# Finer filler, stacks copied by halves and split GpSimd subtractions in a two-layer transformer kernel

## Chip, cores and metric

One core of a Trainium2 chip runs the whole program. The metric is device time in microseconds (us) of one execution; lower is better.

## The reference

Two sequences (batches) of 1024 positions and 512 channels pass through two layers. In each layer both branches read the same normalised input:

```
xn = layernorm(x)
x  = x + causal_attention(xn; Wq, Wk, Wv, Wo) + Wdown(silu(Wgate xn) * (Wup xn))
```

Attention has 16 heads of 32 channels with rotary positions. The feed-forward part (FFN) has 2048 hidden channels in layer 0 and 1408 in layer 1, where its weights are scaled by columns. All is float32. The kernel splits each product into three (high by high, high by low, low by high), each value being held as a rounded high part and a residual low part.

## The kernel before

The order of all work is one list, `STEPS`. Each engine walks it and emits its own part of each step, so the list is the order on every in-order queue, TensorE (PE), VectorE (DVE), ScalarE (ACT), GpSimd (POOL) and SyncE (SP, which issues all DMAs).

The four passes (batch 0 layer 0, batch 0 layer 1, and the same of batch 1) each have an **opening** (normalise and transpose rows 512 to 1023, project the values of all rows and the queries and keys of the first four heads) and four **turns** of four heads each. A turn does, in this order:

- **score stretch one** (`nat` 0 to 15): scores of positions 0 to 511 (half c=0), one matmul each, for four heads. DVE masks and takes the maximum, ACT sums exponentials;
- **score stretch two** (`nat` 16 to 31): half c=1, two matmuls each;
- **weight stretch one** (`st` of sets 0 to 5, with `pv` 0 to 3) and **two** (`st` of sets 6 to 11, `pv` 4 to 9): transposed scores, exponentials by ACT, product with the values, then `wo`;
- the tail, with the last `pv` and the four projections of the next turn's heads (`merge`), in turns 0 to 2. These turns lead into twelve **merged** turns; the other four stand behind openings.

A projected tile passes DVE (L803 to L818), POOL (L715), ACT (the high part, L612) and POOL (the residual, L721). Then SP copies the parts, SBUF to SBUF, into the stacked operands KS and QS with 96 rows, three copies for each of four heads (L564): 12 for the keys, 12 for the queries, each over both halves of the positions. `nat` 0, 4, 8 and 12 wait for the copies of their head, 6 each, on `d_stack0` to `d_stack3` (at L949 and below).

**Filler.** The FFN is cut into pieces (`mlp`, `in_order`) that stand between the attention steps. The digit strings in `PACE` say, step by step, how many pieces stand ahead of each step. Each gate or up product of 12 matmuls is cut into `GU_PARTS` pieces; a down piece has 3 or 6 matmuls.

**Borders.** At the end of layer 0 (`plan`) the rows of half 0 are finished, normalised and transposed (`norms`), with filler between. `v_weights` (POOL L694, 2048 columns in one instruction) stands ahead of the first normalised row. At the end of layer 1 of batch 0 the next batch's x is loaded to `val`; ACT copies it to the residual rows `xres` (`keep`, L592), once the store of the old rows has landed.

Weights pass from a raw buffer through an ACT copy (high part, L654) and a POOL subtraction of 1024 columns (L686); SP then loads the next ones. The wait of `rotate` on SP, by which the stacks are issued:

```
qk = t // NC
sp.wait_ge(sem["g_rl"], n("g_rl", 1))
for h in range(HG):
    for r, src in enumerate(flats):
        sp.dma_start((QS[at, :, h, :] if qk else KS[at, h, :]).bitcast(F32), src[qk][h * DH:(h + 1) * DH, :])
```

Of the kernel before, what the change touches and what calls it, by code (L numbers as in the profile page):

```python
# [20 lines left out]
P = 128  # L21
B, T, D = 2, 1024, 512
H, DH = 16, 32
HG = P // DH
NG = H // HG
KC = D // P
# [30 lines left out]
GU_PARTS = 2  # L57
# [74 lines left out]
def paced(items, pieces, pace):  # L132

    out, k = [], 0
    for steps, digit in zip(items, "".join(pace), strict=True):
        n = int(digit, 36)
# [45 lines left out]
def plan(b, l):  # L182
# [17 lines left out]
    pieces += g0[:GU_PARTS] + late + g0[GU_PARTS:] + g1[:GU_PARTS]  # L200
    if l == 0:
        rows = [piece + [("row", 1, rt)] for rt, piece in enumerate(d0)]
        rows[-1] += normal(1)
        pieces += rows + g1[GU_PARTS:] + output(1) + [piece + [("row", 1, TPC + i)] for i, piece in enumerate(d1)]
        items += norms(1, range(TPC))
    else:
        d0[-1].append(("store", 0))
        d1[-1].append(("store", 1))
        pieces += d0 + g1[GU_PARTS:3 * GU_PARTS]
# [4 lines left out]
        pieces += output(1) + g1[3 * GU_PARTS:] + d1  # L214
# [14 lines left out]
def opening(layer):  # L229
# [9 lines left out]
    out += [values[4], ("rotate", 0), proj[1], values[5], ("rotate", 1), proj[2], values[6], ("rotate", 2), proj[3], values[7],  # L239
# [3 lines left out]
    for k, x in enumerate(out):  # L243
        if x[0] == "open":
# [5 lines left out]
START = [("row", 0, rt) for rt in range(TPC)] + [("stats", 0, 0), ("v_weights", 0), ("xn", 0, 0), ("xn", 0, 1)]  # L250
START += [x for piece in norms(0, range(TPC)) for x in piece] + [("keep", 0)]

PACE = (
    (
        ("00500010101001100112021102021111111020010020010000100100000100100001000010010000010010001001000000000",
         "00700010101001100112021102021111111020010020010000100100000100100001000010010000010010001001000000000",
         "00700010101001100112021201021111111020010020010000100100000100100001000010010000010010001001000000000",
         "007000101010011001120212010211111110200100200000000000000000000000000000000000000000000000006021"),
        ("00500010111110010023030311111111110000000000000000000000000000000000000000000000000000000000000000000",
         "00300010010011001103021021111111111011001001000000100100000000000000000000000000000000000000000000000",  # L260
         "00700010101010011012021202112111111000000000000000000000000000000000000000000000000000000000000000000",
         "0070002000200100110302202111000000000000000000000000000000000000000000000000000000000000000052010"),
    ),
    (
        ("00500010101001100112021201021111111020010020010000100100000100100001000010010000010010001001000000000",
         "00700010101001100112021102021111111020010020010000100100000100100001000010010000010010001001000000000",
         "00700010101001100112021102111111111020010020010000100100000100100001000010010000010010001001000000000",
         "007000101010011001120212010211111110200100200000000000000000000000000000000000000000000000006021"),
        ("00500010111110010023030311111111110000000000000000000000000000000000000000000000000000000000000000000",
# [825 lines left out]
```

## Time and profile before

| | us |
|---|---|
| median of 3 runs | 2059.18 |
| lowest, highest | 2049.17, 2060.20 |
| the profiled execution | 2055.59 |
| its span, first to last instruction | 2053.8 |
| mean granted clock of TensorE | 0.958 of full |

The span is 1.8 us shorter than the profiled execution's own time; the rest lies around it. A line L564 is line 564 of the kernel. PE's busy time counts a matmul from its issue to its modelled end; two matmuls that follow each other closely overlap in it. In the windows view, "(x100)" is the number of instructions in the stretch, "PEclk" the granted clock.

### The profile page before, as it was taken

The numbers are of one execution on the slowest core, as the hardware profiler recorded it, in microseconds if no ns is written. First come the engines' busy times: TensorE is split into PE (matmuls) and PEld (weight loads), VectorE is DVE, ScalarE is ACT, GpSimd is POOL, SyncE is SP. The second block draws the span as 40 slices with busy tenths as digits, with TensorE's granted clock in tenths as the row PEclk, the third lists the DMA queues.
The fourth block names the chain that finished last, engine by engine and source line by source line (L and its number), as shares of the span: only waits on it lengthen the run. The fifth ranks groups of instructions, "written<-read, shape, count | busy, mean of one in ns | idle before, by whom it ended". The sixth has DMA issues, their size and how long they took to land.

```text
span 2053.8 us, 25605 instructions
## 1 busy us (share of the span) xinstructions
PE 1866.4 (91%) x8656; PEld 1347.6 (66%) x8656; DVE 1116.6 (54%) x2432; ACT 1060.1 (52%) x2353; POOL 703.4 (34%) x516
## 2 busy tenths in 40 slices
PE   4999999999899899898889999999988998998987
PEld 3777767775675666656467777776757756575654
DVE  6554647373755564736346465573746636455452
ACT  2464646556256473646425646464652555646363
POOL 3225243242341533333213243534314415233320
PEclk9999999999999899999779999999999999999989
DMA  4213113031130313103213131311401403121201
GB/s 159 67 42 98 42 44 90 27 99 41 52 88 22 87 47 73 42 21 109 72 62 78 37 92 42 84 56 29 122 11 52 101 9 98 42 68 37 66 7 41
DMA packets 59874, 126.20 MB, mean 61 GB/s; under 512 B 9440, under 2 KB 10464, under 8 KB 58720
## 3 DMA queue, kind: packets, MB, share of 16 engines
q1 hardware_dynamic: 59744, 124.57, 22.0%
q8 instruction: 69, 1.13, 0.2%
q14 instruction: 61, 0.50, 0.1%
HBM read 69.48 MB, written 4.19 MB: 36 GB/s over the span
## 4 chain that ended last, share of the span: by engine, by line
PE 69%; DVE 11%; ACT 6%; SPq 5%; issue 5%; POOL 3%; DMA 2%; DVEq 0%; ACTq 0%; POOLq 0%
PE D L905 15%; PE G L905 11%; PE U L905 8%; PE OE L999 7%; PE SS L983 6%; PE OE L905 6%; PE SS L905 6%; SPq L564 5%; PE OE L983 3%; PE OE L962 3%; PE SS L962 2%; DVE OE L826 2%; ACT OE L618 2%; ACT pr L634 2%; DMA QS<-pr 1%
## 5 line engine op out<-in xcount | busy, mean ns | idle before, releaser
L874 DVE TENSOR_TENSOR xres<-D,xres 128x512 f32<-128x512 f32 x352 | 243.1, 691 | 214.1 <-PE D L905 209.7
L634 ACT ACTIVATE pr<-SS 128x512 f32<-128x512 f32 (+3 forms) x512 | 232.2, 501 | 143.8 <-PE SS L983 135.5
L709 POOL TENSOR_TENSOR hl<-tt,hh 128x512 fp32r<-128x512 f32 x108 | 139.0, 1287 | 475.7 <-ACT hh L651 475.7
L618 ACT ACTIVATE OE<-OE,mp 128x384 f32<-128x384 f32 (+3 forms) x256 | 203.4, 795 | 104.9 <-DVE mp L826 104.0
L826 DVE CUSTOM_DVE_ANT_0 OE<-OE,mask 128x384 f32<-128x384 f32 (+3 forms) x256 | 220.5, 873 | 50.6 <-PE OE L962 49.7
L618 ACT ACTIVATE SS<-SS,mp 128x128 f32<-128x128 f32 (+3 forms) x256 | 162.2, 634 | 95.7 <-DVE mp L826 94.0
L728 POOL TENSOR_SCALAR_AFFINE_SELECT pr<-pr 128x512 f32<-128x512 f32 x128 | 81.0, 635 | 378.7 <-ACT pr L634 378.7
L826 DVE CUSTOM_DVE_ANT_0 SS<-SS,mask 128x128 f32<-128x128 f32 (+3 forms) x256 | 167.6, 673 | 64.3 <-PE SS L962 63.0
L905 PE MATMUL G<-xh,wgh 128*128 128x512 f32 x432 | 178.0, 412 | 24.0 <-DVE tt L885 22.8
L983 PE MATMUL SS<-QS,KS 98*128 98x512 f32 (+2 forms) x512 | 182.1, 413 | 14.9 <-ACT pr L634 12.3
L905 PE MATMUL D<-wdh,hh 128*128 128x512 f32 x432 | 174.2, 403 | 19.6 <-DVE xres L874 13.7
L905 PE MATMUL G<-xl,wgh 128*128 128x512 f32 x432 | 171.8, 398 | 0.0
L905 PE MATMUL G<-xh,wgl 128*128 128x512 f32 x432 | 171.3, 397 | 0.0
L905 PE MATMUL D<-wdl,hh 128*128 128x512 f32 x432 | 171.2, 396 | 0.0
L905 PE MATMUL D<-wdh,hl 128*128 128x512 f32 x432 | 170.7, 395 | 0.0
L905 PE MATMUL U<-xh,wuh 128*128 128x512 f32 x432 | 170.5, 395 | 0.0
L999 PE MATMUL OE<-pr,val 128*32 128x512 f32 (+3 forms) x1536 | 168.0, 559 | 2.2 <-POOL pr L728 2.2
L905 PE MATMUL U<-xl,wuh 128*128 128x512 f32 x432 | 169.7, 393 | 0.0
L905 PE MATMUL U<-xh,wul 128*128 128x512 f32 x432 | 169.3, 392 | 0.0
L983 PEld LDWEIGHTS SS<-QS,KS 98*128 98x128 f32 x512 | 98.2, 201 | 96.8 <-ACT pr L634 62.8
L651 ACT CAST hh<-tt 128x512 fp32r<-128x512 f32 x108 | 67.0, 620 | 182.5 <-DVE tt L888 182.5
L634 ACT ACTIVATE pr<-OE 128x512 f32<-128x512 f32 (+3 forms) x256 | 126.2, 493 | 31.4 <-PE OE L983 30.9
(123 smaller groups left out, 3733.6 us busy)
## 6 DMA issues: line engine op xcount, KB each, us to landing
KS<-pr SPq DMA_DIRECT2D x192, 128.0 KB, 2.3
QS<-pr SPq DMA_DIRECT2D x192, 128.0 KB, 2.3
raw<-in_wgate_dram SPq DMA_DIRECT2D x27, 512.0 KB, 3.7
raw<-in_wup_dram SPq DMA_DIRECT2D x27, 512.0 KB, 3.7
raw<-in_wdown_dram SPq DMA_DIRECT2D x27, 512.0 KB, 3.7
raw<-in_wqk_dram SPq DMA_DIRECT2D x16, 512.0 KB, 4.4
val<-in_x_dram SPq DMA_DIRECT2D x4, 1024.0 KB, 6.9
trig<-in_wv_dram SPq DMA_DIRECT2D x4, 1024.0 KB, 5.6
```

The lines of the kernel that those rows point to most:

```text
L564: sp.dma_start((QS[at, :, h, :] if qk else KS[at, h, :]).bitcast(F32), src[qk][h * DH:(h + 1) * DH, :]).then_inc(sem[f"d_stack{h}"], 16)
L618: act.activation(s, s, ACT.Exp, bias=mp[:, c, at:at + 1], scale=-1.0, accum_out=se[:, c, at:at + 1]) \
L634: act.activation(weights(i)[:, h, skip:W], SB[(i * HG + h) % 3][:, skip:W], ACT.Exp, scale=-1.0) \
L651: act.copy(hh[:, fc, :], tt[:, (blk * nfc + fc) % 2, :]).then_inc(sem["a_hh"], 1)
L709: pool.tensor_tensor(hl[:, fc, :], tt[:, (blk * nfc + fc) % 2, :], hh[:, fc, :].bitcast(F32), ALU.subtract) \
L728: pool.affine_select(out=blocks, in_=blocks, pattern=[[0, HG], [1, P]], compare_op=ALU.is_ge, fill=0.0, base=0, channel_multiplier=-1).the ...
L826: dve.tensor_tensor_reduce(s, s, mask[:, NC * W - w_:NC * W], 1.0, 3e38, ALU.add, ALU.min, mp[:, c, at:at + 1]) \
L874: dve.tensor_tensor(xres[:, rt, :], d[:, :], xres[:, rt, :], ALU.add).then_inc(sem["v_dfree"], 1)
L905: ins = pe.matmul(dst, a, b_, start=i == 0, stop=i == len(seq) - 1)
L962: ins = pe.matmul(s[:, part * W:part * W + wide], QS[0:STACK, c, h, qb * P:(qb + 1) * P], KS[0:STACK, h, part * W:part * W + wide], start= ...
L983: pe.matmul(SB[k % 3][:, first:W], KS[0:SHIFT, h, kb * P:(kb + 1) * P], QS[0:SHIFT, c, h, first:W], start=True, stop=True).then_inc(sem["p ...
L999: ins = pe.matmul(O[h * DH:(h + 1) * DH, skip:W], val[:, kb, (n.turns * HG + h) * DH:(n.turns * HG + h + 1) * DH], weights(i)[:, h, skip:W ...
```

## The change

In the words of the code:

- projections run in the order keys c=0, queries c=0, keys c=1, queries c=1. Each is stacked by its own 12 copies as soon as its residual is there, so 48 copies a turn in place of 24, each of half the size. The copies of half 1 count on a new semaphore `d_later`, which `nat` 16 waits for; `nat` 0 waits for those of half 0;
- in the opening the values of rows 5 to 7 stand ahead of the second rotation;
- `GU_PARTS` is 3, and all `PACE` strings are new. The matmuls of filler in each stretch, before and after (the sum of a pass is the same):

| turn | score one | score two | weight one | weight two | tail |
|---|---|---|---|---|---|
| b0 layer 0, t0 | 72, 44 | 102, 88 | 54, 56 | 60, 52 | 12, 12 |
| t1 | 84, 48 | 102, 96 | 54, 60 | 60, 60 | 12, 12 |
| t2 | 84, 52 | 102, 96 | 54, 44 | 60, 66 | 12, 12 |
| t3 | 84, 42 | 102, 108 | 30, 44 | 12, 52 | 96, 204 |
| b0 layer 1, t0 | 72, 48 | 102, 90 | 0, 38 | 12, 20 | 12, 12 |
| t1 | 54, 48 | 108, 96 | 36, 44 | 12, 32 | 12, 12 |
| t2 | 84, 52 | 114, 100 | 0, 44 | 12, 24 | 12, 12 |
| t3 | 84, 42 | 72, 84 | 0, 0 | 12, 12 | 78, 78 |
| b1 layer 0, t0 | 72, 48 | 102, 108 | 54, 44 | 60, 48 | 12, 12 |
| t1 | 84, 36 | 102, 100 | 54, 60 | 60, 60 | 12, 12 |
| t2 | 84, 52 | 102, 96 | 54, 44 | 60, 66 | 12, 12 |
| t3 | 84, 42 | 102, 108 | 30, 44 | 12, 52 | 96, 204 |
| b1 layer 1, t0 | 72, 48 | 102, 90 | 0, 38 | 12, 20 | 12, 12 |
| t1 | 54, 48 | 108, 96 | 36, 44 | 12, 32 | 12, 12 |
| t2 | 84, 46 | 114, 90 | 0, 36 | 12, 48 | 12, 12 |
| t3 | 84, 54 | 72, 72 | 0, 0 | 12, 12 | 78, 78 |

- POOL subtracts 512 columns an instruction: weights in two instructions, the value weights in four. `v_weights` stands behind the third normalised row;
- `keep` is a DMA from HBM on SP's queue in place of ACT's copy; the first add to those rows waits for it;
- the logarithm's first guess is made by ACT in place of DVE; some waits that an earlier one covers are left out.

```diff
-GU_PARTS = 2
+GU_PARTS = 3
...
-            items[-1] += [("x_next",), ("v_weights", 0)]
+            items[-1] += [("x_next",)]
             items += [[("row", 0, rt) for rt in range(TPC)] + normal(0)] + norms(0, range(TPC))
+            items[-3].append(("v_weights", 0))
...
-    out += [values[4], ("rotate", 0), proj[1], values[5], ("rotate", 1), proj[2], values[6], ("rotate", 2), proj[3], values[7],
+    out += [values[4], ("rotate", 0), proj[1], values[5], values[6], values[7], ("rotate", 1), proj[2], ("rotate", 2), proj[3],
...
+            def keep(n, c):
+                sp.wait_ge(sem["d_out"], n("d_out"))
+                sp.dma_start(xres[:, c * TPC:(c + 1) * TPC, :], rows(x, n, c, n.batches)).then_inc(sem[f"d_keep{c}"], 16)
...
             def rotate(n, t):
-                if t % NC < NC - 1:
-                    return
-                qk = t // NC
+                qk, c = t % 2, t // 2
+                cols = slice(c * W, (c + 1) * W)
...
                 for h in range(HG):
+                    done = sem["d_later" if c else f"d_stack{h}"]
                     for r, src in enumerate(flats):
                         at = slice(r * DH, (r + 1) * DH)
-                        sp.dma_start((QS[at, :, h, :] if qk else KS[at, h, :]).bitcast(F32),
-                                     src[qk][h * DH:(h + 1) * DH, :]).then_inc(sem[f"d_stack{h}"], 16)
+                        sp.dma_start((QS[at, c, h, :] if qk else KS[at, h, cols]).bitcast(F32),
+                                     src[qk][h * DH:(h + 1) * DH, cols]).then_inc(done, 16)
...
-                return pool.tensor_tensor(flat(lo), src[:, 0:SIZE[kind]], flat(hi).bitcast(F32), ALU.subtract)
+                for at in range(0, SIZE[kind], W):
+                    part = slice(at, at + W)
+                    ins = pool.tensor_tensor(flat(lo)[:, part], src[:, part], flat(hi)[:, part].bitcast(F32), ALU.subtract)
...
                 elif t == HG * TPC:
+                    pe.wait_ge(sem["d_later"], n("d_later"))
                     pe.wait_ge(sem["a_nat"], n("a_nat", -2))
```

## Rows read from the trace of the kernel before

**Rows 1.** the page, busy us and share of the span of each engine

```profile
PE 1866.4 (91%) x8656; PEld 1347.6 (66%) x8656; DVE 1116.6 (54%) x2432; ACT 1060.1 (52%) x2353; POOL 703.4 (34%) x516
```

**Rows 2.** windows, stretches of one layer 0 turn; columns in the first line

```profile
core 0: us, PE busy (x) PEld busy (x) DVE busy (x) ACT busy (x) POOL busy (x), PEclk, DMA share, GB/s
185.90:208.40 22.50, 22.39 (x100) 18.10 (x101) 15.74 (x43) 12.92 (x37) 10.23 (x7) 1.00 0.71 173
208.40:242.10 33.70, 30.93 (x136) 24.41 (x136) 26.71 (x55) 22.35 (x43) 10.98 (x7) 1.00 0.16 49
242.10:261.90 19.80, 19.80 (x112) 14.96 (x111) 7.21 (x18) 12.97 (x31) 5.05 (x6) 1.00 0.08 27
261.90:288.90 27.00, 27.00 (x145) 18.37 (x143) 6.11 (x9) 14.76 (x31) 9.74 (x8) 1.00 0.11 33
```

**Rows 3.** windows, score stretch one of 12 merged turns: sum

```profile
sum 283.60, PE 259.81 PEld 209.17 DVE 187.75 ACT 157.45 POOL 137.85; mean PE 21.65 PEld 17.43 DVE 15.65 ACT 13.12 POOL 11.49
```

**Rows 4.** windows, first score stretches behind the 4 openings: sum

```profile
sum 78.90, PE 78.46 PEld 63.14 DVE 50.11 ACT 55.08 POOL 31.48; mean PE 19.61 PEld 15.79 DVE 12.53 ACT 13.77 POOL 7.87
```

**Rows 5.** timeline of TensorE, dense stretch; start us, length, form

```profile
517.22 0.39 PE L905 MATMUL D<-wdh,hh 128*128 128x512 f32 x1
...
519.94 0.39 PE L905 MATMUL D<-wdh,hh 128*128 128x512 f32 x1
```

**Rows 6.** the page's DMA issues: copies, KB each, us from issue to landing

```profile
KS<-pr SPq DMA_DIRECT2D x192, 128.0 KB, 2.3
```

**Rows 7.** timeline, GpSimd's first residual and SyncE's stack copies of one turn

```profile
179.21 1.29 POOL L721 TENSOR_TENSOR pr<-pr 128x512 fp32r<-128x512 f32 x1
...
184.60 7.50 SPq L564 DMA_DIRECT2D KS<-pr  x12
192.21 7.71 SPq L564 DMA_DIRECT2D QS<-pr  x12
```

**Rows 8.** timeline of SyncE: copies of 8 KB, and first loads from HBM

```profile
226.58 1.20 SPq L570 DMA_DIRECT2D QS<-mt  x2
...
4.24 0.43 SPq L521 DMA_DIRECT2D val<-in_x_dram  x1
4.72 0.51 SPq L495 DMA_DIRECT2D raw<-in_wqk_dram  x1
```

**Rows 9.** a stall at a stack copy and the stretch behind it

```profile
701.49 0.80 PE L962 MATMUL SS<-KS,QS 96*128 96x256 f32 x2 [7.62 <-DMA QS<-pr]
...
701.50:706.60 5.10, 5.10 (x15) 4.33 (x16) 2.66 (x13) 2.69 (x10) 2.31 (x1) 0.50 0.90 204
```

**Rows 10.** windows, layer 1: weight one, weight two, score two, with sums

```profile
748.10:767.90 19.80, 17.04 (x95) 11.42 (x94) 8.73 (x19) 14.01 (x32) 12.21 (x10) 1.00 0.19 55
...
sum 97.40, PE 84.82 PEld 46.05 DVE 30.11 ACT 71.30 POOL 34.55; mean PE 14.14 PEld 7.67 DVE 5.02 ACT 11.88 POOL 5.76
...
1668.30:1689.90 21.60, 20.16 (x98) 9.70 (x97) 2.77 (x4) 10.64 (x26) 2.54 (x4) 1.00 0.00 1
...
sum 142.40, PE 133.66 PEld 61.16 DVE 16.60 ACT 64.09 POOL 15.23; mean PE 22.28 PEld 10.19 DVE 2.77 ACT 10.68 POOL 2.54
...
942.50:974.10 31.60, 26.13 (x107) 19.26 (x105) 23.19 (x52) 20.75 (x42) 8.13 (x6) 0.93 0.12 34
...
sum 277.30, PE 250.09 PEld 193.86 DVE 215.64 ACT 178.99 POOL 87.89; mean PE 31.26 PEld 24.23 DVE 26.95 ACT 22.37 POOL 10.99
```

**Rows 11.** windows, weight stretches of layer 0's two last turns: sum of 4

```profile
sum 73.00, PE 68.04 PEld 37.04 DVE 15.97 ACT 45.95 POOL 13.93; mean PE 17.01 PEld 9.26 DVE 3.99 ACT 11.49 POOL 3.48
```

**Rows 12.** timeline, VectorE and GpSimd at the start of the kernel

```profile
24.27 5.18 DVE L785 TENSOR_SCALAR pr<-val,mv,st 128x512 f32<-128x512 f32 x2
...
24.42 4.73 POOL L694 TENSOR_TENSOR QS<-trig,QS 128x2048 fp32r<-128x2048 f32 x1 [1.24 <-DVE QS L748]
```

**Rows 13.** timeline, TensorE and ScalarE at two borders of layers

```profile
531.40 0.90 PE L914 MATMUL D<-ident,pr 128*128 128x128 f32 x3 [3.53 <-DVE pr L785]
...
1029.32 1.90 ACT L592 COPY xres<-val 128x2048 f32<-128x2048 f32 x1 [7.53 <-DMA out_dram<-xres]
```

More of the change, by code:

```diff
@@ L199, in plan @@
         g1, d1 = ([[x for x in p if x[0] != "w"] for p in q] for q in (g1, d1))
-    pieces += g0[:GU_PARTS] + late + g0[GU_PARTS:] + g1[:GU_PARTS]
+    pieces += g0[:3] + late + g0[3:] + g1[:3]
     if l == 0:
@@ L203, in plan @@
         rows[-1] += normal(1)
-        pieces += rows + g1[GU_PARTS:] + output(1) + [piece + [("row", 1, TPC + i)] for i, piece in enumerate(d1)]
+        pieces += rows + g1[3:] + output(1) + [piece + [("row", 1, TPC + i)] for i, piece in enumerate(d1)]
         items += norms(1, range(TPC))
+        items[-3].append(("v_weights", 1))
     else:
@@ L282 @@
     "stats": {"v_chain": 13},
-    "keep": {"a_keep": 1},
+    "keep": {},
     "x_next": {"d_x0": 16, "d_x1": 16},
@@ L290 @@
     "nat": {"p_nat": 1, "v_max": 1, "a_nat": 1},
-    "guess": {"v_lse": 2, "a_log": 1},
+    "guess": {"a_log": 2},
     "better": {"v_lse": 3, "a_log": 1},
@@ L318 @@
 SPLITS_OPEN = "ADGU"
-SEMS = sorted({x for a in ADDS.values() for x in a} | {f"raw{k}" for k in range(SLOTS)} | {"g_ds", "d_x0", "d_x1", "d_out"} | {f"d_stack{h}" for h in range(HG)})
+SEMS = sorted({x for a in ADDS.values() for x in a} | {f"raw{k}" for k in range(SLOTS)} | {"g_ds", "d_x0", "d_x1", "d_out"} | {f"d_stack{h}" for h in range(HG)} | {"d_later", "d_keep0", "d_keep1"})
 CREDIT = {s: 0 if s[0] == "d" or s[:3] == "raw" else 1 for s in SEMS}
@@ L580, in store @@
                 sp.wait_ge(sem["v_dfree"], n("v_dfree"))
-                sp.dma_start(rows(out, n, c), xres[:, c * TPC:(c + 1) * TPC, :]).then_inc(sem["d_out"], 16)
-            walk(dict(v_load=v_load, v_weights=v_weights, x_next=x_next, rotate=rotate, flip=flip, w=w, store=store))
+                sp.dma_start(rows(out, n, c, n.b), xres[:, c * TPC:(c + 1) * TPC, :]).then_inc(sem["d_out"], 16)
+            walk(dict(v_load=v_load, v_weights=v_weights, keep=keep, x_next=x_next, rotate=rotate, flip=flip, w=w, store=store))
             sp.wait_ge(sem["d_out"], CREDIT["d_out"] + 16 * NC * B)
@@ L667, in _ @@
             act.wait_ge(s_vconst, 2)
-            walk(dict(keep=keep, norm=norm, values=values, rotate=rotate, nat=nat, guess=guess, better=better, st=st_, heads=heads_,
+            walk(dict(norm=norm, values=values, rotate=rotate, nat=nat, guess=guess, better=better, st=st_, heads=heads_,
                            gate=gate, gated=gated, flip=other_bank, down=other_bank, wo=other_bank, w=w))
@@ L889, in gated @@
                     .then_inc(sem["v_h"], 1)
-            walk(dict(v_weights=v_weights, row=row, stats=stats, xn=xn_, norm=norm, proj=proj, rotate=rotate, nat=nat, guess=guess, better=better, log=log_, flip=flip, heads=heads_, add_wo=add_wo, add_down=add_down, gated=gated))
+            walk(dict(v_weights=v_weights, row=row, stats=stats, xn=xn_, norm=norm, proj=proj, rotate=rotate, nat=nat, better=better, log=log_, flip=flip, heads=heads_, add_wo=add_wo, add_down=add_down, gated=gated))
         @block.tensor
```

129 lines of the change are left out of this document (72 added, 57 removed).

## The prediction

> **What bounds the kernel now.** I read the page first: PE is busy in 91% of the span [rows 1], so what can change is the rest and what PE's work costs. Then the timeline: in a dense stretch twelve matmuls of 512 columns take 519.94 - 517.22 = 2.72 us, 0.227 each [rows 5]. Then windows by stretch. From the length of each I take 0.227 times its filler matmuls; what is left I call its **rest**: attention's own matmuls and all idle or slow time. As a pass has the same filler before and after, the change in time is the sum of the changes in rest. In a layer 0 turn the rests are 22.5 - 84 x 0.227 = 3.5, then 33.7 - 23.1 = 10.6, 19.8 - 12.2 = 7.6 and, with 12 matmuls of a projection also taken off, 10.7 [rows 2]: there PE hardly stands. In layer 1, where filler is short, the six first weight stretches of turns 0 to 2 have a rest of 97.4 - 72 x 0.227 = 81.1, or 13.5 each, and the second ones 142.4 - 144 x 0.227 = 109.8, or 18.3 each [rows 10]. ACT's and DVE's chains set those.
>
> What sets score stretch one is SP. Its copies to the stacks follow one another at (7.50 + 7.71) / 24 = 0.634 us, and each lands 2.3 us after its issue [rows 6, 7]. The turn at T = 185.9 had its first keys ready at 180.5 (179.21 + 1.29), yet its queries were issued from 192.2, because the keys' copies held the queue. The sixth copy that `nat` 0 needs lands at 192.2 + 2 x 0.634 + 2.3 = 195.8, T + 9.9, and the 42 matmuls of filler ahead of it (9.5 us) reach to just that point.
>
> **The stacks, the largest term.** The count of copies doubles. Does a half copy issue in half the time? The rows say no: keys of 128 KB and the 8 KB copies of mt keep the same spacing (two in 1.20 us, 0.60 each) [rows 7, 8]. I take 0.634, as for the nearest kind; the bounds are 0.60 from the smallest copies and, on the other side, 0.634, as nothing here is dearer per piece.
>
> In a merged turn the first residual is ready at T - 5.4. The queue then holds 48 issues: 12 for keys c=0, 12 for queries c=0, and the 24 of half 1. PE makes a projection at least every 24 matmuls (5.4 us), sooner than 12 issues (7.6 us) end, so the queue never runs dry. `nat` 0 needs 15 copies: T - 5.4 + 14 x 0.634 + 2.3 = T + 5.8, where it now starts at T + 9.9. That is the gain that the change has here. But `nat` 16 needs all 48: T - 5.4 + 47 x 0.634 + 2.3 = **T + 26.7**. PE is in order, and has 48 or so matmuls of filler until there (10.9 us) and 3.5 of its own: it would be there at some T + 18, and stands for 8 to 9 us. Before, stretch one ended at T + 22.5 with 84 matmuls of filler done.
>
> Summed: the 12 merged stretches last 283.6, with 948 matmuls of filler, rest 68.7 [rows 3]. After, 12 x 26.7 = 320.4, less 562 x 0.227 = 127.6, rest 192.8. **+124**.
>
> Behind the openings the keys c=0 go out early. The queries c=0 must wait for ACT, which copies the values of row 7 ahead of rotation 1 now: that product ends two projections, 5.4 us, ahead of T, and two ACT copies and a subtraction take some 2.6, so the residual is there at T - 2.8. 36 issues follow: T - 2.8 + 35 x 0.634 + 2.3 = T + 21.7. Before: 78.9, less 288 x 0.227, rest 13.6 [rows 4]. After: 86.8 - 188 x 0.227 = 44.2. **+31**.
>
> **The clock behind the stalls.** One turn shows it: PE stood 7.62 us for a stack copy, and in the 5.1 us behind it the granted clock was 0.50 (1.2 GHz), with 15 matmuls done [rows 9]. That loses up to 2.6 us, 41 over 16 stalls. Nothing is lost where a chain sets the pace anyway, as in much of stretch two; I take 1.5 each, **+24**.
>
> **Filler moved.** It comes out of stretch one (1236 matmuls, then 750) and goes where idle time is.
> - Layer 1, weight stretch one: 36 and 54 matmuls of filler both gave 19.8 us [rows 2, 10], so six stretches with 244 in all last 118.8, rest 63.4: -18.
> - Layer 1, weight stretch two: from 21.6 us at 12 to 27.0 at 60, 0.11 a matmul; at 20, 32, 24, 20, 32, 48 that is 141.5, less 248 (filler and projections) x 0.227, rest 85.3: -24.
> - Layer 1, score stretch two: 277.3 with 792, rest 97.8 [rows 10]. Its chain needs 31.5 (31.6 with only 72 matmuls of filler), which 718 don't lengthen: 252.0 - 162.8 = 89.2: -9.
> - Layer 0, weight stretches of the last turns: 73.0 with 84, rest 54.0 [rows 11]; with 192 about 86.4, rest 42.9: -11.
> - Layer 0 elsewhere gives some filler up: three first weight stretches have 44 for 54 at the same 19.8 us, +7, and a little in the stretches beside them, +2: +9.
>
> **Borders and start.** At the layer 0 border DVE's 5.18 us for two rows stands beside POOL's 4.73 us subtraction at the kernel's start [rows 12]; at the border the same pair left PE standing 3.53 us [rows 13]. The move behind the third row and the four pieces take that and DVE's cast off the path, with 108 more matmuls of filler ahead: -7 each, **-14**. At the layer 1 border ACT stood 7.53 us for the landing of the store before its 1.90 us copy [rows 13]. The wait goes to SP, where the load of the rotary table and weights queue behind it; they are needed only by the next opening, and the second load (4 x 1 MB) is not read before the first add, a stretch later: -5. At the start 4.7 of the 5.18 us go, and DVE's small operations ahead of it wait for half as long an instruction of POOL, 1 us or so: -6. Covers: if `keep` were late, its 1 MB load would be on the path with some 7 us; nothing reads it so soon. The guess on ACT adds a short operation to 32 chains and takes two from DVE; between 0 and 0.3 us each, none of it where PE waits, 0.
>
> **The sum.** +124 + 31 + 24 - 18 - 24 - 9 - 11 + 9 - 14 - 5 - 6 = +101 on the profiled 2055.6 (3.6 under the median of the runs): **2157**.
>
> The Trainium skill ("DMA: Bandwidth & Descriptors", Anatomy of one DMA) gives the sequencer's dispatch of a DMA as some 50 ns and descriptor generation as small (for DMAs that GpSimd issues). As an estimate by that page the 24 more issues would cost 1.2 us a turn, and the time would be the first rival's. The trace disagrees: 0.60 to 0.634 us a copy on SP.
>
> **Rivals.**
> 1. *Issue time follows size*, or is short for these pieces: 0.32 us or less. Then `nat` 16 is free at T + 12 and PE comes later; both sorts of stretch one have the rest of a clean one, 16 x 3.5 = 56 in place of 82.3: -26. No clock loss; the -78 of the other terms stay. 2055.6 - 104 = **1952**. For it: loads from HBM start 0.48 apart [rows 8], so 0.634 is no floor of SP. Against: 8 KB in 0.60. 13%.
> 2. *The spacing is that of the HBM loads*, 0.48. Each 0.1 us less takes 12 x 4.7 + 4 x 3.5 = 70 off, so 0.154 less takes 108 and leaves **2049**, about even. The sign turns at 0.49. 6%.
> 3. *The filler in layer 1's weight stretches brings nothing* (the exponentials, ahead of which it stands in PE's order, come later by what it takes), and each stall costs the full 2.6: +42 + 17 on the forecast, **2216**. Against it: the two stretches with 36 matmuls last 19.8, the four with none (97.4 - 39.7) / 4 = 14.4, so 36 cost 5.4 us, not 8.2 [rows 10]. 9%.
>
> The forecast has 72%. Its own range goes from 2077 (0.60 spacing -24, no clock loss -24, borders and moved filler better by two fifths, -32) to 2210 (clock in full +17, more than half of the moved filler's gain lost, +36). For 8 in 10 I go down to 2065, towards the even case. About 0.5%, 10 us, is what a measurement tells from no change: faster 14% (rival 1 and a little of 2), same 5%, slower 81%.
>
> **What the profile would show.** If right: KS and QS copies x384 each at 0.6 us; the wait of PE at L962's line for a DMA from 19 us to over 120; a gap of 8 to 10 us ahead of the first two-part score in each of 16 turns; the clock at 0.5 behind it; weight stretches of layer 1 at some 20 us; no stop of 3.5 us at the layer 0 border. Wrong: copies at under 0.5 us, or PE reaching `nat` 16 after T + 26, would remove the main term. If stretch one is short and the time still above 2059, it is rival 3's mechanism.

## The result, and the profile after

| | before | after |
|---|---|---|
| median, us | 2057.70 (4 runs) | 2172.88 (4 runs) |
| lowest, highest | 2049.17, 2060.20 | 2170.47, 2173.65 |
| profiled execution, its span | 2055.59, 2053.8 | 2173.65, 2171.9 |
| mean granted clock | 0.958 | 0.933 |

The changed kernel is slower: the ratio is 1.0565 with a 95% interval of 1.0533 to 1.0598. The forecast was 2157, from 2065 to 2215.

The page of the changed kernel: busy times, the shares of the chain that ended last, the line of the scores of `nat` that go to the tile SS, with PE's idle time ahead of them, and the copies to the stacks.

```profile
PE 1882.4 (87%) x8656; PEld 1386.5 (64%) x8656; DVE 1089.6 (50%) x2368; ACT 1057.1 (49%) x2381; POOL 718.8 (33%) x628
...
PE 58%; SPq 20%; DVE 8%; issue 4%; ACT 4%; POOL 4%; DMA 2%; POOLq 0%; DVEq 0%; ACTq 0%
...
L987 PE MATMUL SS<-KS,QS 96*128 96x256 f32 (+2 forms) x384 | 118.0, 381 | 175.4 <-DMA QS<-pr 163.5
...
KS<-pr SPq DMA_DIRECT2D x384, 64.0 KB, 2.0
...
QS<-pr SPq DMA_DIRECT2D x384, 64.0 KB, 2.0
```

PE fell from 91% [rows 1] to 87% of a longer span, with the same 8656 matmuls. 163.5 us of PE's idle time are now ended by a copy to a stack, in 32 waits; before it was 19.3 in 8. By the timeline 106.7 us of them stand at `nat` 16 (4.4 to 9.6 in each of the 16 turns) and 56.9 at `nat` 0. The queue that issues the copies is 20% of the chain, where it was 5%. The copies are twice as many and half as large [rows 6].

The timelines of SyncE and of TensorE over the first merged turn, the one of [rows 7]; start, length, and in brackets the idle time before:

```profile
174.94 7.49 SPq L590 DMA_DIRECT2D KS<-pr  x12
182.53 7.50 SPq L590 DMA_DIRECT2D QS<-pr  x12
190.08 8.20 SPq L590 DMA_DIRECT2D KS<-pr  x12
198.38 7.50 SPq L590 DMA_DIRECT2D QS<-pr  x12
```

```profile
185.81 0.58 PE L987 MATMUL SS<-KS,QS 96*128 96x256 f32 x2 [4.45 <-DMA QS<-pr]
...
207.32 1.01 PE L987 MATMUL SS<-KS,QS 96*128 96x512 f32 x2 [7.66 <-DMA QS<-pr]
```

Score stretch one begins at 178.5. The queue issues 48 copies without a break from 174.9 to 205.9, and PE stops twice: 4.45 us at `nat` 0, which needs the first queries, and 7.66 us at `nat` 16, which needs all 48. In all 16 turns `nat` 16 starts within 0.1 us of the landing of the queue's last copy, 2.0 us after that copy's issue.

The windows of that turn's two score stretches, and the sums of the groups that [rows 3, 4, 10, 11] show of before:

```profile
core 0: us, PE busy (x) PEld busy (x) DVE busy (x) ACT busy (x) POOL busy (x), PEclk, DMA share, GB/s
178.50:207.30 28.80, 16.41 (x65) 12.32 (x63) 14.40 (x41) 14.93 (x41) 14.70 (x12) 0.87 0.42 102
207.30:243.30 36.00, 34.10 (x130) 26.85 (x131) 26.10 (x50) 19.52 (x39) 6.36 (x5) 0.87 0.19 66
```

```profile
sum 343.00, PE 199.61 PEld 154.67 DVE 175.80 ACT 163.59 POOL 140.08; mean PE 16.63 PEld 12.89 DVE 14.65 ACT 13.63 POOL 11.67
...
sum 87.20, PE 58.86 PEld 44.87 DVE 53.01 ACT 51.31 POOL 36.71; mean PE 14.72 PEld 11.22 DVE 13.25 ACT 12.83 POOL 9.18
...
sum 106.70, PE 104.88 PEld 74.55 DVE 38.87 ACT 78.13 POOL 40.26; mean PE 17.48 PEld 12.42 DVE 6.48 ACT 13.02 POOL 6.71
...
sum 141.50, PE 134.62 PEld 77.50 DVE 26.14 ACT 70.89 POOL 30.23; mean PE 22.44 PEld 12.92 DVE 4.36 ACT 11.81 POOL 5.04
...
sum 272.90, PE 252.30 PEld 197.19 DVE 196.81 ACT 166.86 POOL 81.32; mean PE 31.54 PEld 24.65 DVE 24.60 ACT 20.86 POOL 10.16
...
sum 81.80, PE 81.63 PEld 54.94 DVE 28.11 ACT 50.33 POOL 20.38; mean PE 20.41 PEld 13.73 DVE 7.03 ACT 12.58 POOL 5.10
```

They are, in order: score one of the 12 merged turns (283.6 before), of the 4 openings (78.9), layer 1's weight one (97.4), weight two (142.4) and score two (277.3), and the weight stretches of layer 0's last turns (73.0). Less the filler in each, these sums give the rests in the table of the section on why.

At the first border of layer 0, GpSimd (first fence) and TensorE (second):

```profile
579.08 5.06 POOL L720 TENSOR_TENSOR QS<-trig,QS 128x512 fp32r<-128x512 f32 x4 [2.55 <-DVE QS L775]
584.09 2.50 POOL L710 TENSOR_TENSOR wgl<-raw,wgh 128x512 fp32r<-128x512 f32 x2
586.54 1.27 POOL L736 TENSOR_TENSOR hl<-tt,hh 128x512 fp32r<-128x512 f32 x1
```

```profile
587.86 0.50 PE L926 MATMUL D<-wdh,hh 128*128 128x512 f32 x1 [3.38 <-POOL hl L736]
```

The stop of 3.53 us for DVE's row [rows 13] is gone. One of 3.38 us for GpSimd stands in its place (2.98 at the border of batch 1): the value weights' four pieces, and two of the gate weights, are now ahead of the residual `hl` that a down product waits for.

### The profile page after: what moved, and what is told of

Read it like the earlier page. It is cut to its first block, busy times and chain, and to the rows that moved or that the text cites. A ratio compares the mean times of both kernels' runs of the same rounds, so it can differ in the third digit from the quotient of the medians.

```text
span 2171.9 us, 25069 instructions
## 1 busy us (share of the span) xinstructions
PE 1882.4 (87%) x8656; PEld 1386.5 (64%) x8656; DVE 1089.6 (50%) x2368; ACT 1057.1 (49%) x2381; POOL 718.8 (33%) x628
## 4 chain that ended last, share of the span: by engine, by line
PE 58%; SPq 20%; DVE 8%; issue 4%; ACT 4%; POOL 4%; DMA 2%; POOLq 0%; DVEq 0%; ACTq 0%
SPq L590 19%; PE D L926 13%; PE G L926 10%; PE U L926 9%; PE OE L1024 6%; PE SS L1008 5%; PE SS L926 4%; PE OE L926 4%; PE OE L1008 3%; PE SS L987 2%; PE OE L987 2%; DMA QS<-pr 1%; DVE OE L853 1%; DVE xres L895 1%; ACT OE L636 1%
## 5 line engine op out<-in xcount | busy, mean ns | idle before, releaser
L987 PE MATMUL SS<-KS,QS 96*128 96x256 f32 (+2 forms) x384 | 118.0, 381 | 175.4 <-DMA QS<-pr 163.5
L987 PEld LDWEIGHTS SS<-KS,QS 96*128 96x128 f32 x384 | 75.1, 212 | 212.2 <-DMA QS<-pr 177.2
L926 PE MATMUL U<-xh,wuh 128*128 128x512 f32 x432 | 179.7, 416 | 0.0
L926 PE MATMUL G<-xl,wgh 128*128 128x512 f32 x432 | 179.2, 415 | 0.0
L926 PE MATMUL U<-xl,wuh 128*128 128x512 f32 x432 | 178.7, 414 | 0.0
L926 PE MATMUL U<-xh,wul 128*128 128x512 f32 x432 | 178.4, 413 | 0.0
L1008 PE MATMUL SS<-QS,KS 98*128 98x512 f32 (+2 forms) x512 | 171.7, 381 | 7.6 <-ACT pr L655 5.6
L926 PE MATMUL G<-xh,wgl 128*128 128x512 f32 x432 | 178.3, 413 | 0.0
L926 PE MATMUL D<-wdl,hh 128*128 128x512 f32 x432 | 177.0, 410 | 0.0
L1024 PE MATMUL OE<-pr,val 128*32 128x512 f32 (+3 forms) x1536 | 148.9, 505 | 1.0 <-POOL pr L755 1.0
```

The lines of the kernel that those rows point to most:

```text
L926: ins = pe.matmul(dst, a, b_, start=i == 0, stop=i == len(seq) - 1)
L987: ins = pe.matmul(s[:, part * W:part * W + wide], QS[0:STACK, c, h, qb * P:(qb + 1) * P], KS[0:STACK, h, part * W:part * W + wide], start= ...
L1008: pe.matmul(SB[k % 3][:, first:W], KS[0:SHIFT, h, kb * P:(kb + 1) * P], QS[0:SHIFT, c, h, first:W], start=True, stop=True).then_inc(sem["p ...
L1024: ins = pe.matmul(O[h * DH:(h + 1) * DH, skip:W], val[:, kb, (n.turns * HG + h) * DH:(n.turns * HG + h + 1) * DH], weights(i)[:, h, skip:W ...
```

## The experiments

Each kernel ran beside the kernel before on the same chip, and the ratios are against those runs. "Rest" is used as in the prediction.

### The new filler alone (with the small parts)

The changed kernel with projections and stacks in the order of before, 24 large copies a turn. The opening keeps the changed kernel's order:

```diff
-                qk, c = t % 2, t // 2
+                if t % NC < NC - 1:
+                    return
+                qk = t // NC
...
-                        sp.dma_start((QS[at, c, h, :] if qk else KS[at, h, cols]).bitcast(F32), ...)
+                        sp.dma_start((QS[at, :, h, :] if qk else KS[at, h, :]).bitcast(F32), ...)
```

> The changed kernel with the stacks as before: 24 copies a turn over both halves, projections in the old order, all else (filler, borders, halves of GpSimd) as changed. Theory SP queue: score 16 no longer waits for 48 issues of 0.634 us. The first score starts near T + 10, and with 36 matmuls behind it stretch one ends near T + 22 in place of T + 28.8: 12 x 7 = 84 us less, some 13 behind the openings, 10 to 25 of clock: 2050 to 2075. Rival, the moved filler is at fault: stretch one gets no shorter, since only 48 matmuls are there to cover it: 2160 or more.

Measured: 2127.99, ratio 1.0367 (1.0342 to 1.0392). Here I was far off. The fences hold a line of who waited for whom on TensorE, one of its timeline (the stop behind the first opening), the sum of the merged stretches one, and score stretch two of the turn shown above:

```profile
PE SS L984 <- DMA QS<-pr: 153.2, 16, 10.8
```

```profile
77.37 0.58 PE L984 MATMUL SS<-KS,QS 96*128 96x256 f32 x1 [10.63 <-DMA QS<-pr]
```

```profile
sum 315.30, PE 199.68 PEld 157.82 DVE 166.77 ACT 148.23 POOL 132.35; mean PE 16.64 PEld 13.15 DVE 13.90 ACT 12.35 POOL 11.03
```

```profile
207.40:239.40 32.00, 29.92 (x131) 23.51 (x131) 26.64 (x52) 21.23 (x44) 6.71 (x6) 1.00 0.17 50
```

The large copies leave SP no earlier than before, but the strings of the change put at most 12 matmuls of filler ahead of `nat` 0 (the third digit), where before 42 stood in most turns. So PE stops once in each of the 16 turns, 8.5 to 10.8 us, at `nat` 0, and never at `nat` 16. The new strings fit only stacks that are ready early, and lose about as much as the new stacks do. The last fence bears on the clock: the same stretch two, with the same filler, lasts 32.0 us at a granted clock of 1.00 here and 36.0 at 0.87 in the changed kernel, where a stop at `nat` 16 stands right ahead of it.

### The new stacks alone

The kernel before with 48 half copies, the new projection order, the opening's new order, the wait of `nat` 16, and the changed kernel's waits of the first four scores:

```diff
-                if t % NC < NC - 1:
-                    return
-                qk = t // NC
+                qk, c = t % 2, t // 2
+                cols = slice(c * W, (c + 1) * W)
...
                 elif t == HG * TPC:
+                    pe.wait_ge(sem["d_later"], n("d_later"))
```

> The kernel before with the new stacks alone (48 half copies, order keys and queries of half 0 first, score 16 waits for the last), its own filler strings kept, so 84 matmuls stand ahead of score 16. Theory SP queue: stretch one ends at T + 28.5 however full it is, where it ended at T + 22.5 to 25: 12 x 5 = 60, behind the openings 4 x 2 = 8, clock 5 to 20: 2115 to 2150. Rival, the loss comes from taking filler away from there: with 84 in place the time is within 10 us of before, about 2058.

Measured: 2153.84, ratio 1.0495 (1.0461 to 1.0528), just above the range. The waits of TensorE and of GpSimd, then the sum of the merged stretches one:

```profile
PE SS L967 <- DMA QS<-pr: 63.9, 14, 6.4
...
POOL raw L703 <- DMA raw<-in_wdown_dram: 61.4, 5, 18.0
```

```profile
sum 332.90, PE 261.71 PEld 208.99 DVE 199.62 ACT 167.47 POOL 132.37; mean PE 21.81 PEld 17.42 DVE 16.64 ACT 13.96 POOL 11.03
```

With the old filler (54 to 84 matmuls) the stop at `nat` 16 is 3.5 to 6.4 us in the merged turns, and the rest of their stretches one is 118.0, not 215.6. The copies also hold back what is behind them on SP: GpSimd waits 61.4 us for weights, against 16.7 before.

### Two by two, with the small parts in all four

The small parts are GpSimd's pieces, `keep` by DMA, ACT's guess, the place of `v_weights` and the waits left out. `small_parts` is the changed kernel with old stacks, old opening order, `GU_PARTS` 2 and the old strings; `stacks_small` has the new stacks and opening on top. `old_stacks` has the new opening order, so in the table's first row that order changes with the filler, and in the first column with the stacks.

```diff
-GU_PARTS = 3
+GU_PARTS = 2
...
-    out += [values[4], ("rotate", 0), proj[1], values[5], values[6], values[7], ("rotate", 1), ...
+    out += [values[4], ("rotate", 0), proj[1], values[5], ("rotate", 1), proj[2], values[6], ...
```

> The changed kernel with the stacks, the opening's order, the cut into 2 parts and all filler strings as before. What is left of the change: GpSimd subtractions in halves, value weights prepared behind the third row, residual rows by a second load, the guess on ScalarE, the left-out waits. My sum gives these -6 at the start, -14 and -5 at the borders; the trace of the changed kernel gives -6 at the start, about 0 and -2 at the borders and, which I had not forecast, -11 in the tails. Forecast 2030 to 2045 against some 2054 before. Rival, that the tails got shorter by the new filler ahead of them: 2045 to 2052.

> The changed kernel with the filler strings and the cut into 2 parts as before, so new stacks and small parts with the old filler: the fourth corner beside the changed kernel (2173), old_stacks (2128, new filler, old stacks) and small_parts. If stacks and filler added up, it would be 2173 - (2128 - small_parts), some 2080. Theory: each of the two alone leaves TensorE waiting for the stack copies, and together they share one wait, so that they don't add: new_stacks measured 2154 without the small parts, less some 15: 2130 to 2142.

| with the small parts | old filler | new filler |
|---|---|---|
| old stacks | 2027.57 (0.9872, 0.985 to 0.9894) | 2127.99 (1.0367) |
| new stacks | 2124.40 (1.0343, 1.032 to 1.0367) | 2172.88 (1.0565) |

Both new kernels came out a little under their ranges. The small parts are a gain of some 26 us. By the ratios the stacks alone then cost 97 us, the filler alone 102 and both together 142: they don't add up, because they make PE stop for the same thing, the end of the queue of copies. The wait of `stacks_small`, and the merged sums of `small_parts` and of it:

```profile
PE SS L987 <- DMA QS<-pr: 63.5, 15, 5.6
```

```profile
sum 285.00, PE 261.52 PEld 210.52 DVE 187.01 ACT 158.11 POOL 141.20; mean PE 21.79 PEld 17.54 DVE 15.58 ACT 13.18 POOL 11.77
```

```profile
sum 332.80, PE 261.04 PEld 208.66 DVE 198.84 ACT 167.63 POOL 135.91; mean PE 21.75 PEld 17.39 DVE 16.57 ACT 13.97 POOL 11.33
```

The same PE work lasts 47.8 us longer with the new stacks. Most of the other half of their 97 lies right behind the stops: the score stretches two have 34 more rest (90.2 for 76.1 in layer 0, 112.4 for 92.3 in layer 1), and their mean granted clock is 0.93 for 0.98. The openings with their first stretch have 10 more.

### Twelve of the copies issued by ACT

If the spacing on SP's queue is the limit, a second queue must help. ACT issues the queries of half 1, one ahead of each exponential from `nat` 4 on:

```diff
+                if t == 3:
+                    return
...
+                if 4 <= t < 16:
+                    hh_, r = divmod(t - 4, 3)
+                    if t == 4:
+                        act.wait_ge(sem["g_rl"], n("g_rl"))
+                    act.dma_start(QS[r * DH:(r + 1) * DH, 1, hh_, :].bitcast(F32), ...).then_inc(sem["d_later"], 16)
```

> The changed kernel with the 12 copies of the queries of half 1 issued by ScalarE, one ahead of each of the exponentials 4 to 15; SyncE issues 36. Theory SP queue: the last SyncE copy lands at T - 3.6 + 35 x 0.634 + 2.0 = T + 20.6, stretch one 8 us shorter in each of 12 turns and about 6 behind the 4 openings, clock 15: 2173 - 135 = 2040, if ScalarE's issues (0.6 each, 7 a turn) don't lengthen the chain of exponentials; if they do in full, 7 x 16 = 112 comes back and it is 2150. Rival, copies are limited by the DMA engines and not by SyncE: no gain, 2170.

Measured: 2107.72, ratio 1.027 (1.0233 to 1.0307): by the ratios some 60 us under the changed kernel, where I had forecast 133. PE's waits, and ACT's and PE's timelines in the turn shown above, whose stretch one begins at 175.8 here:

```profile
PE SS L995 <- DMA QS<-pr: 109.3, 31, 6.8
```

```profile
185.71 0.51 ACTq L640 DMA_DIRECT2D QS<-pr  x1
...
199.10 0.51 ACTq L640 DMA_DIRECT2D QS<-pr  x1
```

```profile
204.58 1.01 PE L995 MATMUL SS<-KS,QS 96*128 96x512 f32 x2 [5.95 <-DMA QS<-pr]
```

SP's part ended at 196.25, but PE waited to 204.58, so this turn's stretch one is as long as before the edit (28.8 us). There are two reasons. ACT's copies go out only as its exponentials come, from 185.7 on, and those depend on PE's own scores: the last one goes at 199.1. And it lands 5.4 us after its issue, not 2.0, beside three weight loads that SP, free earlier, has put in flight by then. The DMA issues from 176 to 196 us (first line) and from 196 to 200:

```profile
QS<-pr ACTq DMA_DIRECT2D x7, 64.0 KB, 2.0
...
QS<-pr ACTq DMA_DIRECT2D x6, 64.0 KB, 4.6
```

Over the 12 merged turns the last copy lands 2.0 to 7.1 us after its issue, 4.0 in the mean, and 4.0 or more only where two or three loads have gone out ahead of its landing (no run moves the loads by themselves); in the changed kernel those loads queue behind the 48 copies, and it is 2.0 in every turn. So the issues on SP's queue are what bound `nat` 16 in the changed kernel: with 12 of them moved, PE's stops there fall from 106.7 to 53.4 us, where by the rival, the DMA engines as the limit of the copies, nothing would have come. My 2040 was too low because I had counted neither the exponentials nor the weight loads.

### More filler ahead of `nat` 16

To hide the stop, 30 matmuls of each layer 0 turn of `stacks_small` (8 turns) moved from score stretch two to ahead of `nat` 16. Turn 1's string, its part that changes:

```diff
-"00700010101001100112021102021111111020010020...
+"00700010101002211212021101010001111020010020...
```

> stacks_small (2124.4) with 30 matmuls of filler moved in each of the 8 turns of layer 0 from score stretch two (102 to 72) to ahead of score 16, which waits for the 48 copies. Theory: in the merged turns of layer 0 TensorE is then busy until about T + 29, so the wait there is covered, the clock stays up, and stretch one's rest falls from some 8 to 4; but stretch two falls to its chain's 31.5 us, where its rest rises by 5. Wait for the copies down by 25 us or more in the records, time only 0 to 20 us less, 2104 to 2124. Rival, the stall is a fixed cost of this arrangement whatever stands ahead of it: no change of the wait either.

Measured: 2162.67, ratio 1.051, far above the forecast. PE's wait, and the stretches one and two of turn 1 and the stretch two of turn 3, in `stacks_small` (first fence) and in this kernel (second):

```profile
PE SS L987 <- DMA QS<-pr: 34.4, 8, 5.4
```

```profile
183.00:209.40 26.40, 22.39 (x100) 18.05 (x100) 16.51 (x44) 13.75 (x39) 10.61 (x9) 0.98 0.42 102
209.40:244.90 35.50, 33.73 (x136) 26.51 (x136) 25.85 (x51) 21.69 (x42) 11.40 (x10) 0.92 0.20 68
...
455.50:490.60 35.10, 34.01 (x136) 26.40 (x137) 25.88 (x51) 21.71 (x42) 11.39 (x10) 0.92 0.29 96
```

```profile
189.40:218.50 29.10, 29.10 (x131) 23.88 (x132) 19.03 (x48) 13.96 (x38) 10.57 (x9) 1.00 0.45 115
218.50:251.40 32.90, 26.67 (x106) 19.71 (x105) 24.12 (x47) 22.17 (x44) 11.45 (x10) 0.95 0.19 56
...
466.00:506.40 40.40, 32.17 (x107) 23.96 (x106) 23.95 (x48) 22.35 (x44) 11.42 (x10) 0.75 0.24 83
```

The wait fell from 63.5 to 34.4 as expected, and the rest of the merged stretches one from 117.9 to 88.0. The time went up all the same, by some 34 us. Thirty matmuls out of stretch two are 6.8 us. In turn 1 the stretch got 2.6 shorter, in turn 3 it got 5.3 longer, and the eight of layer 0 together went from 275 us to 285 with 54 us less filler: their rest rose from 90.2 to 154.9. PE's scores, DVE's maxima and ACT's exponentials take turns there, and with less filler PE stands between them. In turn 3 it stops 4.67 us ahead of a gate product that waits for DVE, then 1.88 and 1.39 for ACT, and half of the stretch runs at the lower clock. The mean granted clock of the eight stretches fell from 0.95 to 0.84; as an estimate, (1 - clock) times the length, what the clock takes rises from 14 to 46 us, half of the 65. Why turn 3 fares so much worse than turn 1, with the same filler, was not looked into.

### Filler moved in the best kernel

The same question asked of `small_parts`: 24 matmuls out of score stretch two of turns 1 and 2 of layer 1, in turn 1 to the start of stretch one, in turn 2 to weight stretch one, where before there was none.

```diff
-"00300010010011001103021021111111111011001001...
+"00700010010011001101011020111111111011001001...
```

> small_parts (2027.6) with filler moved in four turns of layer 1: in turns 1, 24 matmuls from score stretch two (108 to 84) to ahead of the first score, where TensorE stands 7.6 us for the stack copies; in turns 2, 24 from score stretch two (114 to 90), which lasts 39 to 40 us with them, into weight stretch one (0 to 24). Theory, filler is worth something only where TensorE waits and costs nothing only where a chain does not: turns 1 give 5 each less a shorter saving in stretch two (33.3 to 31.5 and no more) and 2 to 3 of clock, turns 2 give 8 less 4: -10 to -20, 2008 to 2018. Rival, filler is worth the same anywhere: 2025 to 2030.

Measured: 2033.07, ratio 0.9887 (0.9865 to 0.9909), no gain over 0.9872, where I had forecast 10 to 20 us. Windows of score stretch two, of turn 1 and of turn 2 of batch 0, and PE's one stop in turn 1's stretch one:

```profile
709.20:740.90 31.70, 27.43 (x119) 21.00 (x118) 24.40 (x51) 21.18 (x44) 5.06 (x4) 1.00 0.07 21
...
820.80:856.30 35.50, 30.70 (x124) 23.04 (x123) 27.25 (x49) 23.35 (x45) 15.16 (x12) 0.95 0.20 60
...
690.10 0.79 PE L924 MATMUL G<-xh,wgh 128*128 128x512 f32 x1 [6.73 <-POOL wgl L708]
```

In turn 2 the 5.4 us of filler gone made the stretch 3.6 shorter (39.1 before the edit), and the weight stretch took the 24 matmuls in 16.5 us, where it had lasted 16.6 with none (14.4 in batch 1, so 2.1 came back there). In turn 1 stretch two fell only from 33.0 to 31.7, while stretch one, which took them in, rose from 25.7 to 30.1. The stop of 7.65 us for the copies did go, but one of 6.73 stands in its place: the filler that moved ahead needs its gate weights earlier than GpSimd has made their residual. The two turns cancel.

### The small parts one by one

GpSimd's pieces alone, on the kernel before:

```diff
-                return pool.tensor_tensor(flat(lo), src[:, 0:SIZE[kind]], flat(hi).bitcast(F32), ALU.subtract)
+                for at in range(0, SIZE[kind], W):
+                    part = slice(at, at + W)
+                    ins = pool.tensor_tensor(flat(lo)[:, part], src[:, part], flat(hi)[:, part].bitcast(F32), ALU.subtract)
+                return ins
```

> The kernel before with GpSimd's subtractions in pieces of 512 columns alone, the value weights' preparation left in its old place. Theory: it frees VectorE ahead of the first rows at the start (3 of the 5.6 us) and at the borders (3 each), and shortens stalls in the score stretches, of whose shortening small_parts showed 5 to 10 us in layer 0 and 4 in layer 1: 2035 to 2046. Rival, what small_parts gained came from moving the preparation behind the third row and from the second load, and pieces cost GpSimd a start each: 2050 to 2056.

Measured: 2040.2, ratio 0.9927 (0.9899 to 0.9955). DVE's first rows and GpSimd's pieces at the start of this kernel, to be held against [rows 12]:

```profile
20.84 2.89 DVE L790 TENSOR_SCALAR pr<-val,mv,st 128x512 f32<-128x512 f32 x2
24.99 1.38 DVE L790 TENSOR_SCALAR pr<-val,mv,st 128x512 f32<-128x512 f32 x1
...
24.82 5.31 POOL L698 TENSOR_TENSOR QS<-trig,QS 128x512 fp32r<-128x512 f32 x4
```

DVE's row no longer waits out 4.73 us; one beside the pieces takes 1.38. The pieces cost GpSimd 18 us in all (721.3 busy for 703.4), where it is a third busy. The rest at the two layer 0 borders fell from 24.0 to 16.6: of PE's two stops for DVE's rows, 3.26 and 3.53 us at the first border, the second is gone and the first stays (3.25).

`small_parts` with the guess of the logarithm back on DVE:

```diff
-    "guess": {"a_log": 2},
+    "guess": {"v_lse": 2, "a_log": 1},
```

> small_parts with the guess back on VectorE. I had costed its move to ScalarE at 0. Theory: 0, within 3 us of 2027.6. Rival: score stretch two got shorter (57.5 of rest for 62.8 in layer 0, 63.4 for 67.5 in layer 1) by two VectorE operations and their handshakes less: 2032 to 2040.

Measured: 2035.74, ratio 0.9902 (0.9878 to 0.9926), against 0.9872. The intervals overlap, so the times alone don't tell the two apart. The sums of layer 0's eight score stretches two, `small_parts` first and this one second, with the same matmuls, stand apart:

```profile
sum 260.90, PE 249.19 PEld 195.29 DVE 211.75 ACT 179.67 POOL 91.11; mean PE 31.15 PEld 24.41 DVE 26.47 ACT 22.46 POOL 11.39
```

```profile
sum 268.20, PE 249.51 PEld 195.38 DVE 213.50 ACT 179.03 POOL 91.12; mean PE 31.19 PEld 24.42 DVE 26.69 ACT 22.38 POOL 11.39
```

Their rest is 76.1 with the guess on ACT and 83.2 with it on DVE. The other traces with the old filler and old stacks fall in line: 83.0, 83.8 and 82.9 with it on DVE, 76.2 with it on ACT.

The repeated waits left out, alone, on the kernel before:

```diff
-                act.wait_ge(sem["p_pv"], n.at("p_pv", i - RING + 1))
+                if h == 0:
+                    act.wait_ge(sem["p_pv"], n.at("p_pv", i - RING + 1))
```

> The kernel before with only ScalarE's repeated waits left out (one per set and per pair of chunks in place of one per head and chunk). Theory: they were met long before, and cost ScalarE's sequencer some tens of ns each, 400 or so of them, in stretches where its chain sets the pace: 0 to 8 us less than before. Rival, they explain the shorter weight stretches of the changed kernel in layer 1 (17.9 us at 44 matmuls of filler where I had 19.8), with 10 us or more.

Measured: 2053.21, ratio 0.9988 (0.9968 to 1.0008). Nothing that can be told from zero. The edit leaves out 628 waits (576 in `st`, 52 in `gated`), not 400; each takes 17 ns in ACT's trace, 10.7 us of its queue's time in all, and next to none of it was on the path.

The value weights back ahead of the first row at layer 0's borders, in the changed kernel and in `small_parts`:

```diff
-    return [("stats", layer, 0), ("xn", layer, 0), ("xn", layer, 1)]
+    return [("stats", layer, 0)] + [("v_weights", 1)] * layer + [("xn", layer, 0), ("xn", layer, 1)]
```

> The changed kernel with the value weights' preparation back ahead of the first normalised row at the two layer 0 borders; the layer 1 border and start as changed. My forecast of -7 at each of these borders did not come (rest 11.8 and 11.8 against 12.1 and 11.9). Theory: its four GpSimd pieces now stand ahead of the FFN's residual and weight residuals, and TensorE stops 3.4 us for those. Back in the old place this stop goes and the stop at the second transposed row returns: within 3 us of the changed kernel, 2170 to 2176. Rival: the move did bring 5 to 7 us each and something else took it; then 2183 to 2187.

> As small_parts, with the value weights' preparation at the two layer 0 borders back in its old place, now in four GpSimd pieces. In the changed kernel this gave 3.6 less (2169.3 against 2172.9). Theory: in the new place its pieces hold up GpSimd's residual for the next down product. 2 to 5 us less than small_parts; rival, with the old filler there is other work ahead of that product and it is even.

Measured: 2169.25, ratio 1.0563 (1.0535 to 1.0592), and 2026.39, ratio 0.9863 (0.9839 to 0.9886). Neither time can be told from its partner's. In the traces the rest of the two borders goes from 23.6 to 19.3 in the first and from 18.7 to 17.5 in the second, so the step's move gave nothing once the pieces were small, and cost 4.3 us in the changed kernel. There, without the move, the stop for `hl` is gone at both borders and the first stop for DVE's row is 3.20 us, for 2.23 with it. `small_vw` is the best kernel found: 1.4% under the kernel before.

## Why the prediction was right, and where it was off

The direction, the main mechanism (48 issues on SP's queue, `nat` 16 waiting for the last) and the range held. That the number came within 16 us is in part luck: the errors of the terms below add up to some +55 and -38. By the prediction's own terms, from the rests of the two kernels (us; the clock's +24 was kept apart in the forecast, and its +9 for the rest of layer 0 is set down as +8 and +1):

| term | before, after | measured | forecast |
|---|---|---|---|
| stretch one, merged | 68.7, 215.6 | +147 | +124 |
| stretch one, openings | 13.6, 44.6 | +31 | +31 |
| score two, layer 0 | 83.0, 98.5 | +15 | +1, and clock |
| score two, layer 1 | 97.8, 110.1 | +12 | -9, and clock |
| weight one, layer 1, turns 0 to 2 | 81.1, 51.4 | -30 | -18 |
| weight two, layer 1, turns 0 to 2 | 109.8, 85.3 | -24 | -24 |
| weight stretches, layer 0, last turns | 54.0, 38.3 | -16 | -11 |
| weight stretches, layer 0, others | | +5 | +8 |
| layer 0 borders | 24.0, 23.6 | -0.4 | -14 |
| layer 1 border and the end | 33.2, 32.0 | -1 | -5 |
| start | 35.0, 28.2 | -7 | -6 |
| tails | 26.2, 15.4 | -11 | none |
| weight stretches, layer 1, last turns | 67.6, 60.7 | -7 | none |

With 2.6 more in the openings this is the +118 by which the span grew; the forecast had +101.

**What bounds the kernel, and the stacks: right.** The step "does a half copy issue in half the time? The rows say no" carried the forecast. The 48 copies of the turn shown take (205.88 - 174.94) / 48 = 0.645 each, the first 12 of them (182.53 - 174.94) / 12 = 0.63; forecast was 0.634. Rivals 1 and 2 needed 0.32 and 0.48, and fall with it. The estimate by the 50 ns of dispatch in the Trainium skill ("DMA: Bandwidth & Descriptors", Anatomy of one DMA) falls as well. `nat` 16 came at T + 28.8, where the forecast had T + 26.7. Over the twelve merged turns (mean length 343.0 / 12 = 28.6) the first copy went out at T - 3.5 in ten and T - 5.2 in two, T - 3.8 in the mean and not T - 5.4; the mean spacing was 0.647, above the 0.634 that the prediction called its upper bound; and the last copy landed after 2.0 us, not 2.3. Twelve times 1.6 + 0.6 - 0.3 makes the 23 that the term was short. About half of it is no loss: T comes earlier because the tails are shorter, and they give 11 back.

**The attribution: incomplete.** The term was put under "The stacks", but it counted the change in rest, so it held the removal of filler as well. The two by two shows both halves: with the old filler, the new stacks leave the merged rest at 117.9; it is the new filler that raises it to 215.6. Its other side, that the new strings would lose some 100 us without the new stacks too, I didn't see, although the prediction says that the 42 matmuls ahead of `nat` 0 "reach to just that point". I also named one stop a turn; there are two, the one at `nat` 0 up to T + 7.3 where the forecast had T + 5.8.

**The clock: right in kind, mis-sized.** +24 was taken at 1.5 us for each of 16 stalls, with "Nothing is lost where a chain sets the pace anyway, as in much of stretch two". Score two rose by 27 where +1 and -9 were forecast without the clock, so some 36. The mean granted clock of the 16 stretches two is 0.90, where it was 0.98 before; as an estimate, (1 - clock) times the length, the clock takes 54 us there in place of 9. It is the stop right ahead of stretch two that does it, not the number of stops: `old_stacks`, with the same filler and its stops at `nat` 0 only, has rests of 81.4 and 91.9 there at a clock of 0.97, which is the forecast without the clock, while `stacks_small`, with the old filler and in most turns one stop, at `nat` 16, has 34 more there than `small_parts`.

**Filler moved: right, and rival 3 refuted.** Weight one of layer 1 took 36 to 44 matmuls in 16.1 to 19.2 us, mean 17.8, where the forecast had 19.8 from turns with 36 and 54 in two pieces. The granted clock of the six stretches is 1.00 throughout, where the four without filler had 0.76 and 0.88 before; the prediction had no term for that. With `GU_PARTS` 3 the pieces are of 4 matmuls; that finer ones fit the chain better was not tried by itself. Weight two is as forecast. Rival 3's first half (this filler brings nothing) falls: 54 us came back there.

**Borders: the failed step.** "The move behind the third row and the four pieces take that and DVE's cast off the path": -14 forecast, -0.4 found. Only half of it was there to win: the pieces alone, on the kernel before, give 7.4 us for both borders, and of PE's two stops for DVE's rows take off the second. The move shortens the first by only 1.0 us (3.20 to 2.23), and puts GpSimd's five microseconds ahead of the residual `hl`. PE stops 3.38 and 2.98 us for it, and the clock falls behind the stop; without the move the same kernel has 4.3 us less at the borders. The few microseconds left between these two figures, in a kernel whose filler differs as well, are not traced. I had costed what the move frees on DVE and not what it delays on GpSimd's own queue. The layer 1 border gave 2.3 of 5 us; `keep` was not tried by itself. The guess, costed at 0, is worth some 6 us by the ratios and 7 in layer 0's stretches two by the traces: its chain on DVE does lie in score stretch two, where the chains set the pace.

**Not forecast: the tails, -11.** Before, each next turn began with a down piece, which waited 1.64 us for DVE's add; the new strings begin with gate or up pieces. The traces with the new filler all have the shorter tails, those with the old filler all have the old ones, `small_parts` too. **And layer 1's last turns, -7**, with no filler either way.

## What to carry to other kernels

Count the issues on a queue, not the bytes: at the 0.63 us a copy that both sizes took here, cutting a copy in two to have the first half early doubled the time until the last one is out, and what stood behind it on that queue, weight loads too, came later. Filler that covers a wait is part of that wait's price: when operands are restaged and filler is replaced in one step, cost each alone and both together, for here +97 and +102 made +142. A second queue helps less than its share of the issues if it frees the first to start large loads that the last copies then share the DMA engines with. Filler is not free to move either: where a chain of three engines paces a stretch, taking filler out of it saved less than the filler's own time here, and in `cover` made the stretches longer, at a lower granted clock. Cutting long GpSimd instructions beside VectorE work was the cheap gain (0.7% alone).

## What the runs showed of the hardware

- SyncE issues a copy from SBUF to SBUF every 0.63 us whether it moves 64 KB or 128 KB, and ACT's queue mostly takes 0.51 to 0.56 us for one (a few 0.65 to 1.55); with the landing 2.0 and 2.3 us after the issue, halving a copy saved 0.3 us of latency and no issue time. With three weight loads in flight (256 and twice 512 KB) the same 64 KB copies landed 3.7 to 5.4 us after the issue (`act12`, from 196.3 us on).
- A VectorE row beside one GpSimd subtraction of 2048 columns took as long as that (two rows in 5.18 us beside 4.73), and one row 1.38 us beside subtractions of 512 columns (0.53 with GpSimd idle), which took 1.29 to 1.35 each in the mean. The Trainium skill ("SBUF — State Buffer", two separate sides) says that the pair of ports is held for the whole instruction and the loser blocks; the trace agrees.
- Behind a stop of 3.38 us TensorE's matmuls came to be 0.42 us apart, against 0.23 ahead of it: the lower of its two levels, 1.2 GHz. The timeline of the changed kernel at the layer 0 border:

```profile
583.63 0.40 PE L926 MATMUL D<-woh,ah 128*128 128x512 f32 x1
583.86 0.39 PE L926 MATMUL D<-wol,ah 128*128 128x512 f32 x1
...
590.61 0.63 PE L926 MATMUL D<-wdh,hl 128*128 128x512 f32 x1
591.03 0.63 PE L926 MATMUL D<-wdh,hh 128*128 128x512 f32 x1
```
